# A decoder layer on one core: every step of the five engines placed anew by a new table of times

## The reference, cut to what matters

```python
x = _layernorm(x + _L0_attn_ref(x, w_gate, w_down, w_a, w_i, w_v, ...))      # recurrence + gate/down network
x = _layernorm(x + _L0_xattn_ref(x, ctx, ctx, mask, Wq, bq, Wk, bk, Wv, bv, Wo, bo))
x = _layernorm(x + _L0_ffn_ref(x, k0, k1, k2, s0, s1, s2))
...
Q, K = apply_rope(Q, cos, sin), apply_rope(K, cos, sin)                      # x * cos + x2 * sin
attn = softmax(where(mask == 0, neg_inf, Q @ K.T * SCALE)); out = attn @ V @ Wo.T + bo
```

## Time and profile before

| | before |
|---|---|
| time, median of 3 runs | 865.04 us (864.85 to 865.87) |
| time of the profiled execution | 863.57 us |
| its span | 861.8 us |
| mean granted TensorE clock | 0.975 |
| PE busy | 770.2 us (89%) |
| DVE busy | 657.7 us (76%) |
| ACT busy | 597.8 us (69%) |
| POOL busy | 381.2 us (44%) |

### The profile page before, as it was taken

One profiled execution on the slowest core, in us unless ns is written; L12 is line 12 of the kernel. 1 busy time (PEld: TensorE's weight loads), 2 busy tenths in 40 slices (PEclk: granted clock), 3 DMA queues, 4 the chain that ended last, 5 costly groups with the idle time before them and its releaser, 6 DMA issues.

```text
span 861.8 us, 18693 instructions
## 1 busy us (share of the span) xinstructions
PE 770.2 (89%) x7150; PEld 551.3 (64%) x7184; DVE 657.7 (76%) x1218; ACT 597.8 (69%) x983; POOL 381.2 (44%) x582
## 2 busy tenths in 40 slices
PE   1786667899999999999999999998999999999996
PEld 0443324768676767677676768675767677676675
DVE  5665858688888879796988888887969698867252
ACT  7665564786869595959687686958695968754721
POOL 6987523336162543454453615354445445230010
PEclk9999859999999999999999999999999999999998
DMA  9002120111202020202111121202030201111000
GB/s 304 3 13 63 36 75 2 52 37 39 62 26 76 14 75 14 76 26 68 33 51 50 36 66 26 75 14 75 14 88 14 74 16 43 35 36 42 2 13 25
DMA packets 53033, 40.73 MB, mean 47 GB/s; under 512 B 7345, under 2 KB 52433, under 8 KB 52945
## 3 DMA queue, kind: packets, MB, share of 16 engines
q1 hardware_dynamic: 52944, 39.53, 15.7%
HBM read 26.66 MB, written 12.59 MB: 46 GB/s over the span
## 4 chain that ended last, share of the span: by engine, by line
PE 50%; DVE 26%; ACT 13%; issue 7%; POOL 3%; SPq 0%; DMA 0%; ACTq 0%; DVEq 0%; POOLq 0%
PE bankC L1355 15%; PE bankA L1292 7%; DVE nmax L1662 5%; PE bankC L1339 4%; PE slotB L1279 4%; PE bankA L1206 3%; PE slotB L1261 3%; PE bankA L1138 2%; ACT pr L992 2%; PE bankC L1371 2%; ACT L992 2%; DVE bn L1618 2%; DVE x L1626 2%; DVE sg L1537 2%; DVE qt L1650 2%
## 5 line engine op out<-in xcount | busy, mean ns | idle before, releaser
L1355 PE MATMUL bankC<-h0h,w 128*128 128x256 f16 x1024 | 232.9, 273 | 0.5 <-DVE h0l L1711 0.5
L1355 PE MATMUL bankC<-h0l,w 128*128 128x256 f16 x1024 | 231.9, 273 | 0.0
L1662 DVE TENSOR_REDUCE nmax<-slotB 128x4 f32<-128x1024 f32 x128 | 154.7, 1213 | 5.6 <-PE slotB L1261 4.0
L992 ACT ACTIVATE pr<-slotB,mcol,cscale 128x1024 f32<-128x1024 f32 x128 | 146.1, 1204 | 3.9 <-PE slotB L1279 3.4
L1355 PEld LDWEIGHTS bankC<-h0h,w 128*128 128x128 f16 x1024 | 100.2, 98 | 34.4 <-issue 20.2
L1355 PEld LDWEIGHTS bankC<-h0l,w 128*128 128x128 f16 x1024 | 100.2, 98 | 13.4
L1711 DVE SCALAR_TENSOR_TENSOR h1l<-bankC,h1h 128x512 f16<-128x512 f32 x64 | 43.7, 684 | 45.7 <-ACT h1h L1021 45.7
L1292 PE MATMUL bankA<-pr,v_aug 128*32 128x256 f32 x1024 | 71.1, 397 | 0.0
L1711 DVE SCALAR_TENSOR_TENSOR h0l<-bankC,h0h 128x512 f16<-128x512 f32 x64 | 43.9, 688 | 35.5 <-ACT h0h L1021 35.1
L1339 PE MATMUL bankC<-xh,w 128*128 128x256 f16 x256 | 60.0, 276 | 3.7 <-DVE xl L1705 2.3
L724 POOL TENSOR_SCALAR rstd<-mv 128x2 f32<-128x2 f32 x48 | 9.6, 200 | 117.3 <-DVE mv L1621 116.3
(11 more groups left out here) (273 smaller groups left out, 1873.1 us busy)
## 6 DMA issues: line engine op xcount, KB each, us to landing
x<-in_x SPq DMA_DIRECT2D x16, 256.0 KB, 2.9
cT<-in_ctxT SPq DMA_DIRECT2D x16, 256.0 KB, 3.1
scr<-kpart SPq DMA_DIRECT2D x16, 256.0 KB, 2.3
scr<-qpart SPq DMA_DIRECT2D x16, 256.0 KB, 2.4
k_st<-scr SPq DMA_DIRECT2D x32, 128.0 KB
q_st<-scr SPq DMA_DIRECT2D x32, 128.0 KB, 2.8
out<-x SPq DMA_DIRECT2D x16, 256.0 KB, 2.1
k_st<-scr SPq DMA_DIRECT2D x32, 64.0 KB
```

What stands on the lines that cost most here:

```text
L992: act.activation(pr[i % 2][:, c, :, :].rearrange("p h s -> p (h s)"), slotB[ringB.slot(g, name)][:, :], ACT.Exp, scale=cscale[:, g, 0:1], ...
L1355: ins = pe.matmul(bankC[ringC.slot(g, name)][:, e * T:(e + 1) * T], w_1[:, i // 2, (2 * m + e) * P:(2 * m + e + 1) * P], (h0h, h0l)[i % 2] ...
L1662: dve.tensor_reduce(nmax[:, 0:H * NT].rearrange("p (a q b n) -> p q n a b", a=2, q=NHG, b=2)[:, hg, n], slotB[ringB.slot(g, name)][:, :].r ...
```

## The change

The two tables get new numbers, and nothing else in the program is touched. All instructions stay, with their operands; what changes is in which order an engine runs them, and which of two PSUM slots an item uses. Two of the lines (the diff changes every line of both tables; `out` and the remaining steps likewise):

```diff
@@ TIMES, "queries"
-        x1T P64.632 A66.163 V67.416 | xb G72.897 | q P68.744 A71.927 | rotq G70.318 V72.422
-        qp A74.116 V78.059 | qput S34.707 | qget S55.241""",
+        x1T P64.724 A66.96 V69.418 | xb G66.737 | q P67.483 A71.535 | rotq G73.751 V75.686
+        qp A75.13 V77.572 | qput S42.047 | qget S68.136""",
```

More of the change, by code:

```diff
@@ L79 @@
-        w:wk G33.3 A37.618 | w:wk2 G40.046 | w:wv G36.6 A36.672 | w:wv2 G45.86 | w:wq G47.517 A56.34
-        w:wq2 G63.18 | w:wo G70.907 A86.391 | w:wo2 G90.597""",
-    "recurrent": """
[L82 to L88, removed]
+        w:s V-474.955 P-9.401 | w:m V-102.802 A-461.195 P14.721 | w:a V3.711 | w:iv V14.889
@@ new lines @@
+    "recurrent": """
+        loadx S34.511 | scale A0.692 G-1.733 V-2.178 | stat1 G9.838 | round V12.391
+        xqT P13.194 A14.826 | iv0 P18.276 A23.506 V25.935 | iv1 P23.223 A24.948 V26.99
+        a P15.632 A19.744 | aT P18.151 A22.579 | sq A28.63 | ivT P27.476 V34.242 | cum V35.123
+        recur V36.407 | rec P34.122 A34.633 V36.594 | max2 V37.596 | stat2 G35.574 | round2 V38.013
+        rqT P39.928 A42.085 | gate0 P41.609 A45.283 V47.812 | gate1 P42.003 A46.345 V48.948
+        stat3 G49.058 | round3 V50.618 | sqT P51.114 A53.363 | down P54.384 V56.622 | bn V58.209 G59.924
+        x1 V62.109""",
@@ L89 @@
     "keys": """
-        loadc S-3.757 | kT P35.28 A37.097 | v P45.368 A47.612 | rotk G40.223 | kp A47.502 G57.624
-        kput S15.095 | kget S43.44""",
+        loadc S9.966 | kT P37.177 A39.477 | v P46.733 A46.619 | rotk G39.86 | kp A44.827 G57.986
+        kput S25.373 | kget S33.075""",
     "context": """
-        cn A10.259 P19.898 V22.895 G30.719 | cs G31.734 A33.165 | cl G37.784 | cg G39.912""",
+        cn A13.005 P20.76 V26.287 G27.842 | cs G29.368 A33.811 | cl G32.669 | cg G41.671""",
@@ L100 @@
-        score7 P106.069 V110.372 | max P111.933 A113.887 V116.938 | maxrow S68.494""",
+        score0 P90.364 V92.824 | score1 P91.448 V94.633 | score2 P93.188 V96.793
+        score3 P93.553 V98.165 | score4 P97.457 V100.478 | score5 P102.346 V104.07
+        score6 P105.703 V106.796 | score7 P106.422 V110.449 | max P112.076 A115.195 V119.506
+        maxrow S80.93""",
     "values": """
-        exp0.0 P117.24 A122.787 | exp0.1 P117.25 A123.299 | pv0 P122.433 | exp1.0 P120.638 A124.187
-        exp1.1 P122.393 A124.191 | pv1 P123.763 A129.759 | exp2.0 P122.65 A124.34
@@ L104 @@
-        exp2.1 P123.953 A125.436 | pv2 P126.193 | exp3.0 P124.567 A125.604 | exp3.1 P126.003 A127.126
-        pv3 P129.303 A130.822 | oTok P131.948 V136.594 | oT P135.051 A137.017 V138.173
-        wo P139.646 V141.166 | bn2 V142.24 G143.869 | x2 V145.999""",
-    "network": """
[L108 to L115, removed]
+        exp0.0 P115.964 A120.629 | exp0.1 P116.003 A120.662 | pv0 P122.109 | exp1.0 P118.763 A120.879
@@ new lines @@
+        exp1.1 P120.894 A121.699 | pv1 P123.617 A127.538 | exp2.0 P122.388 A122.004
+        exp2.1 P123.754 A124.181 | pv2 P125.854 | exp3.0 P124.398 A124.483 | exp3.1 P125.831 A126.307
+        pv3 P128.027 A130.541 | oTok P132.043 V136.304 | oT P134.963 A137.123 V138.185
+        wo P139.505 V141.268 | bn2 V142.279 G144.82 | x2 V146.054""",
+    "network": """
+        x2T P144.967 A144.227 V147.713 | l0_0 P149.329 A148.522 V153.756
+        l0_1 P151.588 A154.144 V156.34 | l0_2 P152.971 A157.123 V158.655 | l0_3 P154.81 A158.98 V160.209
+        l1_0.0 P156.384 | l1_0.1 P157.246 | l1_0.2 P160.724 | l1_0.3 P162.913 A166.375 V171.486
+        l1_1.0 P164.813 | l1_1.1 P165.634 | l1_1.2 P165.698 | l1_1.3 P166.005 A173.528 V175.92
+        l1_2.0 P168.556 | l1_2.1 P173.003 | l1_2.2 P173.493 | l1_2.3 P175.436 A178.122 V180.101
+        l1_3.0 P178.421 | l1_3.1 P180.652 | l1_3.2 P182.738 | l1_3.3 P186.828 A189.705 V190.186
+        l2.0 P189.642 | l2.1 P191.913 | l2.2 P192.554 | l2.3 P194.335 V199.556 | bn3 V218.955 G214.582
+        out A228.917 | store S210.477""",
@@ L119 @@
     "weights": [0],
[L120 to L125, removed]
@@ L132 @@
-    "network": [3.233, 50.714, 99.585, 147.433, 195.455, 242.845, 291.211, 339.448,
-                387.489, 435.702, 483.038, 531.38, 580.428, 630.43, 682.309, 728.915],
+    "recurrent": [4.209, 53.164, 94.095, 142.515, 191.798, 239.883, 288.297, 336.769,
+                  384.578, 432.684, 481.356, 529.482, 578.16, 625.991, 675.086, 723.942],
+    "keys": [13.595, 46.299, 103.507, 154.904, 203.474, 251.111, 298.43, 348.035,
+             395.164, 443.072, 492.772, 540.449, 588.677, 638.229, 687.029, 735.528],
@@ new lines @@
+    "context": [7.735, 38.587, 77.278, 149.876, 197.911, 225.525, 273.859, 342.991,
+                369.553, 418.288, 466.598, 533.994, 562.657, 630.026, 659.717, 708.367],
+    "queries": [3.065, 51.043, 91.769, 140.327, 188.957, 237.24, 285.791, 334.051,
+                382.08, 431.025, 478.759, 527.392, 574.583, 623.969, 672.764, 724.617],
+    "scores": [6.104, 41.947, 89.838, 139.235, 187.248, 235.624, 283.915, 332.234,
+               379.695, 428.757, 476.856, 525.254, 573.241, 622.564, 671.822, 722.083],
```

35 lines of the change are left out of this document (16 added, 19 removed).

## The result

| | before | after |
|---|---|---|
| median of 4 runs each | 865.36 us (864.85 to 865.87) | 852.71 us (851.50 to 855.70) |
| ratio | | 0.9859, 95% interval 0.9832 to 0.9886 |
| the same, in a later comparison (17 and 6 runs) | 864.30 us (860.80 to 866.53) | 854.97 us (853.78 to 856.58) |
| ratio there | | 0.9899, 95% interval 0.9873 to 0.9925 |
| the profiled execution, its span | 863.57 us, 861.8 us | 855.70 us, 853.9 us |

The change is faster by 12.7 us in the first comparison and by 9.3 us in the second. The forecast was 852.8. The two profiled executions lie 7.9 us apart, so the forecast's sum of 12.2 agrees with the first pair of medians better than with the traces. The account behind the experiments shows which of its terms held and which did not.

The account below looks back on a forecast made before the run. TensorE, busy 89% of the span, was taken as the bound. Terms -6.1, -3.1, -1.3 and -1.7 sum to -12.2: 851.4 us against the profile's 863.6, hence median 852.8; own range 849.5 to 856.5, 8 in 10 from 847 to 861.

Parts of the forecast that it names:

- `kp` and `xb` ahead of `rotq`: GpSimd order: VectorE's addition L1650 takes 0.69 us instead of 1.53, ending TensorE's waits at `exp1.0`; -6.1 us.
- first and second rivals: First: ScalarE keeps `exp0.0` late, 858.9 us, chance 0.14; second: median-length GpSimd steps make `rotq` 1.24 us late, 869, chance 0.08.
- my own rule, median lengths: Each GpSimd step keeps its median length, so the three ahead of `rotq` start it 1.2 us late.
- `bn` behind `score7`: VectorE order: GpSimd's `cs` then begins after `x1` began, so TensorE's waits at `x1T` go; -3.1 us.
- Keys first: DMA order: keys fetched first and context last, so `score0` no longer waits for the keys; -1.3 us.
- `score4` and the gates: TensorE order: `round3` and `rotk` meet in six of 12 periods as before; 0 us, bounds -5.6 and +5.4.
- `gate1` ahead of `oTok`: TensorE swap of neighbours: `oTok` 0.4 us later, needed by VectorE just then; 0 us, or about 0.1 us if uncovered.
- The warning sign that I named: A long `round3` in more than eight periods, from `gate1` having made `oTok` late, would show the prediction wrong.
- my upper bound: For `score4` and the gates: `round3` and `rotk` meeting in all periods, +6 x 0.9 = +5.4 us.
- The start: Group 1: `x1` and L1650 get shorter on the chain to the first exponentials; -1.7 us, weight shuffle 0 within 3 us.
- its five lines: TensorE's waits `exp1.0`, `x2T`, `iv1`, `x1T` and `score0`, 20 us in 640, hold whatever steady reordering can bring.
- fourth rival: Start, 100 to 140 us at mean clock 0.70: it shifts 4 us either way, 849 or 857; chance 0.17.

Follow-up runs that it names:

- e5: The kernel before with `xb`, `kp` and the next group's `cl` on GpSimd moved ahead of `rotq`: 856.62 us, ratio 0.9910.
- e3: The kernel after with `xb` and `kp` on GpSimd put back behind `rotq` in groups 3 to 14: 857.20 us, ratio 0.9938 to before.
- e4: The kernel before with only `xb` and `kp` on GpSimd moved ahead of `rotq` in groups 3 to 14: 861.80 us, ratio 0.9985.
- e10: The kernel before with only VectorE's `bn` moved behind `score7` in periods 3, 4, 8, 9 and 12: 862.32 us, ratio 0.9977.
- e8: The kernel before with SyncE fetching keys ahead of queries and loading a context behind both, periods 2 to 14: 862.67 us, ratio 0.9984.
- e2: The kernel after with TensorE's `gate1` put back behind `l1_3.1` in periods 2 to 13: 851.29 us, ratio 0.9874 to before.
- e1: The kernel after with GpSimd's `rotk` also waiting for VectorE's `round3` from group 2 on: 845.48 us, ratio 0.9806 to before.
- e6: The kernel before with GpSimd's `rotk` also waiting for VectorE's `round3` from group 2 on: 857.27 us, ratio 0.9920.

## Why the prediction came out right, and where it was not

**`kp` and `xb` ahead of `rotq`, -6.1: right.** The addition fell to 0.69 us, `rotq` was not late, the waits went. e5 does this part alone and gets 5.6 us, some of it eaten by a late `rotq` in periods 6 and 10; e3 undoes `xb` and `kp` and loses 0.5 us per group in the mean. One thing in the wording was loose: e4 shows that moving the two steps of the heading does almost nothing while `cl` takes their place. The first and second rivals were wrong: nothing else held `exp0.0`, and the three steps ran at their lowest, as the rule that the prediction cites from the Trainium skill ("SBUF — State Buffer", "Who interferes with whom") would have it; my own rule, median lengths, did not hold.

**`bn` behind `score7`, -3.1: right mechanism, 2.3 by e10.** The rest of the 3.1 was one wait of 0.9 us in period 1, which belongs to the start. In e10 it is there as well, and it is missing in e4 and e8, which have the order of the kernel before in that place. Period 9 had `bn` ahead too and lost nothing; `cn` stood behind there, which fits e10's theory, though no run moves `cn` in that period alone.

**Keys first, -1.3: right in this trace** (e8, 1.4), but the number is that of one run. The traces of other kernels with the keys last show 0 to 2.4 us.

**`score4` and the gates, 0: the step that failed.** I counted which of `score4` and `gate0` comes first and found six and six. What decides is when `kb` is ready, measured from `round3`, and this moved by 0.05 us in every period through the edit that I had costed at nothing, `gate1` ahead of `oTok`: "If that cover is gone it costs the 0.1 us or so that it is late." `oT` was not late but early, and the six meetings cost 4.3 us by e2, which undoes this edit alone, and 4.8 us by the same six periods in e1. The warning sign that I named ("a long `round3` in more than eight periods") was right; the reason I gave there (`gate1` having made `oTok` late) was not, since `rden`, VectorE's first step behind `oTok`, begins at 6.52 us of the period before and at 6.53 after. In the profiled run my upper bound, a meeting in every period, is what happened, though at less than its 5.4 us. The reading behind the term was wrong in a second point: by e6 the meetings did not fill the waits of `x2T`.

**The start, -1.7: mis-sized, and mostly noise.** The first score of period 2 came at 176.1, 176.8, 176.9, 177.1, 179.2 and 180.2 us in the six traces that have the order of the kernel before there (e8 but for the keys of group 2), and at 176.9, 177.1, 177.4 and 178.5 in the four with after's order and no wait added. The means differ by 0.2 us (177.7 and 177.5). So the start varies by 4.1 us between traces of the same order. The profiled execution of the kernel before, and e10's, have the two longest; 2.2 us of the 7.9 between the profiles come from there. What the shorter `x1` and addition of group 1 brought by themselves is not shown: no run makes that change alone.

**The end, not looked at: +0.5 us.** There TensorE waits for VectorE's `xl` 0.9 us, where it waited 0.6, and once more for VectorE (L1717) 0.3 us.

**The sum.** By traces: -5.6 (e5), -1.4 (e8), -2.3 (e10) and +4.3 (e2) make -5.0 us for the steady part, where -6.2 was measured. The rest of 1.2 us is about what e5 still waited there before `exp1.0`: 1.3 us in periods 2, 6 and 10, each behind a `rotq` that was 0.6 to 1.2 us late. After has no such wait. This last step is a sum and not an experiment. The waits themselves give the same total by other parts. In the steady part TensorE waited 20.1 us before and 13.8 after. The waits of `exp1.0` (5.8), of `x1T` (2.1) and for the keys (1.3) went, `x2T` rose from 4.6 to 10.0, and 2.4 us of smaller waits went too, mostly for VectorE in periods 6, 7 and 13. The prediction had left these out, where it said that whatever a reordering can bring is in its five lines.

**The range.** Its stated reason, 3 us to each side, gives 849.8 to 855.8 and not 849.5 to 856.5; nothing hangs on the difference.

**Why the medians then agree.** In part by luck. The four first runs of the kernel before were 864.85 to 865.87, all at the long end of the 860.3 to 866.8 that 54 later runs of it span. Measured beside 17 of those, the change is worth 9.3 us. Three of the four runs of after were 2.6 to 4.2 us faster than the profiled one; fewer meetings (each up to 0.9 us) or another start could explain that, but no trace of those runs is there, so it stays open. What the fourth rival had said, that the start goes its own way by 4 us with the clock, turned out true of single runs (below) and not of the change.

## What to carry to other kernels

An instruction that shares something with another engine has two prices, and the margin between them can be a few hundredths of a microsecond. So for each such pair near the path, read from the trace how far it is from meeting, and ask of every edit ahead of either whether it moves one of them; an edit "at no cost" that brought them 0.05 us closer made six meetings, 4.3 us together. Where the margin is thin, a semaphore that puts the two behind each other can be worth nearly as much as a new order: here one wait brought 8.5 us, and the whole new order 9.3. And when you name the step that disturbs another, name the place, not the step: the one that moves up into it disturbs just the same.
